# GATv2 edge scores summed by TensorE with the channels on the partitions, in a four-layer graph network on one Trainium2 core

## The chip, the core and the metric

The kernel runs on one NeuronCore of one Trainium2 chip. The metric is the device time of one execution in microseconds (us). Three runs of the kernel before are known.

## The reference, cut to what matters

3125 nodes with 256 channels, 50000 edges (sorted by target node) and one loop edge per node. Four graph layers follow one another, each with a residual sum and a layer norm. Layer 0 is the one that the change is about: two GATv2 convolutions, the first with 2 heads of 64 channels, the second with 2 heads of 128.

```python
def gatv2_conv(x, src, dst, Wl, Wr, att, b, heads, c_out):
    xl = (x @ Wl).reshape(n, heads, c_out)
    xr = (x @ Wr).reshape(n, heads, c_out)
    e = jax.nn.leaky_relu(xl[src] + xr[dst], NEG_SLOPE)      # 0.2
    logit = jnp.einsum('ehc,hc->eh', e, att)
    m = jax.ops.segment_max(logit, dst, num_segments=n)
    a = jnp.exp(logit - m[dst])
    denom = jax.ops.segment_sum(a, dst, num_segments=n)
    alpha = a / denom[dst]
    out = jax.ops.segment_sum(alpha[:, :, None] * xl[src], dst, num_segments=n)
    return out.reshape(n, heads * c_out) + b
```

Layer 1 is a GAT layer with 8 heads, layer 2 a graph transformer of three sublayers, layer 3 a sum over neighbours with a two-layer network. All arithmetic is float32.

## The kernel before, in words

The edges are first sorted into slots: 464 tiles of 128 slots, so that the two tiles of a group point to target nodes of one block of 128 nodes. `edge_pass(kind, table, width)` (L828) is then called seven times: twice as "gatv2" (pass 1 with width 128, pass 2 with width 256), once as "gat", three times as "hgt", once as "gin". A pass works through 232 groups of 2 tiles; 8 groups are a batch, of which there are 29.

The order is written out by hand. Every engine runs the same sequence of slots, one slot per group, and in slot n it does stage s for group n minus the lag of s (`LAG`): one_hots 0, turn 1, target 2, logit 3, weigh 14, add_up 15, keep 16. Once in a batch come the softmax stages LOGITS (10), IN_TILE and TURN_LOGITS (11), ACROSS (12) and POWERS (13). Engines wait for each other by semaphores, so that an engine that falls back by more than about a slot holds the others.

In a "gatv2" pass before, for each group:

- GpSimd (POOL) gathers the two tiles of source rows with an indirect DMA each (L943). It waits until the rows of two batches ago are weighed.
- VectorE (DVE) makes two one-hot tiles, slot by target node (L852).
- TensorE (PE) transposes both (L968, L969) and ScalarE (ACT) copies them to `spreads` (L1034).
- TensorE puts target row plus source row into PSUM, slots on the partitions and channels on the free axis: for each tile a matmul of `spreads` with the block's 128 target rows in `qtab` (L981) and one of the identity with the gathered rows (L984).
- ScalarE writes 0.2 times that sum to SBUF (L1039); VectorE takes the larger of both (L1124), which is the leaky relu, and then for each tile and head multiplies by `att` and sums the channels (L1187, with a second instruction that reads the accumulator).
- After the softmax, ScalarE multiplies the source rows by their weights, a tile and head at a time (L1074, four per group), and writes the weights beside them (L1080).
- TensorE sums weighted rows over the slots of each target (L1020), and VectorE adds the result to `acc` (L1213).

Once in a batch: VectorE copies the scores to `logits` (L1246), TensorE turns them (L962) so that lanes of heads and tiles lie on the partitions, VectorE runs four scans (L1148, L1149, L1165, L1167) for the maximum of each segment and subtracts it (L1177), ScalarE takes the exponential (L1050), TensorE turns the weights back (L1006). TensorE and VectorE each load 8 block numbers from `block_of` into registers.

"gat" and "hgt" passes have the same structure, but ScalarE makes the one-hots there, and VectorE weighs the rows (L1108).

Of the kernel before, what the change touches and what calls it, by code (L numbers as in the profile page):

```python
# [18 lines left out]
ALU = mybir.AluOpType  # L19
# [4 lines left out]
P = 128  # L24
# [3 lines left out]
NP = NT * P  # L28
# [11 lines left out]
BIG = 2.0 ** 100  # L40
PADSEG, PADLOC, PADDST = 9999.0, 999.0, 4000
# [23 lines left out]
def gnn_kernel(nc, A, out):  # L65

    ctx = ExitStack()
    with ctx:
# [10 lines left out]
        tab_l0a, tab_l0b, tab_l1 = dram("tab_l0a", (NP, 128)), dram("tab_l0b", (NP, D)), dram("tab_l1", (NP, D + H))  # L79
# [4 lines left out]
        seg_dram = dram("seg_dram", (1, T * P + 2))  # L84
        hid_dram = dram("hid_dram", (8, P, NP))
# [23 lines left out]
        qtab = arena[:, QTAB:QTAB + NT * D].rearrange("p (j c) -> p j c", j=NT)  # L109
# [574 lines left out]
        def load_slots():  # L684

            q4 = T // 4
            segT = arena[0:q4, 0:4 * P].rearrange("p (q s) -> p q s", q=4)
            with nc.Block() as block:
                @block.sync
                def _(sp):  # L690
                    sp.dma_start(slots_i.rearrange("p t f -> p (t f)"),
                                 rec_dram[:, :].rearrange("(p t) f -> p (t f)", p=P)).then_inc(loaded.sem, 16)
                    sp.wait_ge(placed.sem, placed.at(2))
# [5 lines left out]
                    sp.wait_ge(loaded.sem, loaded.at(16 * 7))  # L699

                @block.vector
                def _(dve):
# [6 lines left out]
                    dve.wait_ge(multiplied.sem, multiplied.at(4))  # L709
                    dve.tensor_copy(segT, PS[0][0:q4, :].rearrange("p (q s) -> p q s", q=4)).then_inc(placed.sem, 1)  # L710
                    dve.wait_ge(step.sem, step.at(5))
                    dve.wait_ge(placed.sem, placed.at(1))
# [8 lines left out]
            loaded.base += 16 * 7  # L721
            step.base += 5
            placed.base += 2
            multiplied.base += 4
# [96 lines left out]
        names = ("oh_made", "oh_turned", "spread_made", "target_spread", "activated", "leaked", "multiplied_rows", "raw_made",  # L821
# [3 lines left out]
        S = {n: sig(n) for n in names}  # L825
        arrived = [[sig(f"arrived{a}{k}") for k in range(BG)] for a in range(2)]

        def edge_pass(kind, table, width):  # L828
# [7 lines left out]
            index = slot_typed if hgt else slot_src  # L836
            pot = [PS[0][:, 0:GT * P], PS[1][:, 0:GT * P]]
            z = [PS[2][:, :].rearrange("p (t c) -> p t c", t=GT), PS[3][:, :].rearrange("p (t c) -> p t c", t=GT)]
            sums = [PS[4][:, 0:wc], PS[5][:, 0:wc]]
            plt, pcols, pscale = PS[6][:, 0:P], PS[6][:, P:P + 33], PS[6][:, 192:192 + H]  # L840
            pat = PS[7][:, 0:P].rearrange("p (h t) -> p h t", h=H)
# [4 lines left out]
            w_dve = gat or hgt  # L846
# [54 lines left out]
            with nc.Block() as block:  # L901
# [20 lines left out]
                def _(pool):  # L922
                    freed = S["summed"] if gin else S["weighted_made"]

                    def batch_fn(s, a, use):
# [8 lines left out]
                        for k in range(BG):  # L934
# [3 lines left out]
                            if not gin:  # L938
# [11 lines left out]

                @block.tensor
# [1179 lines left out]
```

## Time and profile before

| | |
|---|---|
| three runs | 8071.43, 8066.46, 8066.6 us; median 8066.6 |
| span of the profiled execution | 8071.7 us, which is taken as its own time (the profile gives no other) |
| busy share of the span | PE 75%, DVE 64%, ACT 39%, POOL 46% |
| pass 1 (gatv2, width 128), first to last scan | 943.6 to 1587.6 us |
| pass 2 (gatv2, width 256), first to last scan | 1708.5 to 2507.6 us |

Busy shares are means over stages with different limits, so the two gatv2 passes are read by themselves. Busy time of PE also overstates its load, since matmuls overlap in the pipeline: the distance between starts in the timeline is what a matmul takes from the next one. Each float32 matmul shows as two MATMUL records with two weight loads; a transpose shows as one.

### The profile page before, as it was taken

Reading aid. Unit: us, or ns where it says so; the run is one execution under the profiler, and the core shown is the slowest. Engines: PE = TensorE matmul, PEld = TensorE weight load, DVE = VectorE, ACT = ScalarE, POOL = GpSimd, SP = SyncE. Lnnn points to the kernel's source line nnn. Section 1 sums busy time; section 2 is a strip of 40 time slices with the busy share of each in tenths; the row PEclk is TensorE's granted clock in tenths of the full one; section 3 lists DMA queues with packets and bytes.
Section 4 is the critical chain, followed back from the end, with each engine's and each line's share of the span. In section 5 each row is a group of like instructions: output and inputs, shape, how many; then the busy total and the mean of one; then the engine's idle time right before and its main releaser. Section 6 shows DMA issues by size and latency. Waiting matters only on the chain. (4 is left out here: it accounts for less than half of the span.)

```text
span 8071.7 us, 142182 instructions
## 1 busy us (share of the span) xinstructions
PE 6039.7 (75%) x30254; PEld 4802.6 (59%) x30255; DVE 5203.4 (64%) x17428; ACT 3149.5 (39%) x10642; POOL 3712.1 (46%) x3878
## 2 busy tenths in 40 slices
PE   2786577778885788597887897886897886837676
PEld 1665466657774566385665785665785665724455
DVE  7664588768887566538997438997428997343313
ACT  0111266546663466325553225553225553300015
POOL 0676377545552577307662007662006662047740
PEclk9999999899997688698998999998998998955668
DMA  1000211322222233326663026663026663023330
GB/s 28 3 3 10 49 47 47 37 74 74 72 74 38 80 98 98 64 96 184 174 177 87 1 95 185 174 177 88 1 94 182 176 174 92 1 88 96 97 67 16
DMA packets 306945, 689.96 MB, mean 85 GB/s; under 512 B 95900, under 2 KB 135510, under 8 KB 306390
## 3 DMA queue, kind: packets, MB, share of 16 engines
q0 software_dynamic: 209536, 581.61, 28.1%
q1 hardware_dynamic: 81264, 98.11, 3.7%
q10 hardware_dynamic: 15846, 7.19, 0.3%
q14 instruction: 226, 1.85, 0.1%
q8 instruction: 73, 1.20, 0.1%
HBM read 605.77 MB, written 80.89 MB: 85 GB/s over the span
## 5 line engine op out<-in xcount | busy, mean ns | idle before, releaser
L943 POOL DMA_INDIRECT arena<-tab_l,idx x2320 | 2327.5, 1003 | 967.6 <-issue 578.5
L1020 PE MATMUL bank<-arena,onehots 128*128 128x264 f32 (+3 forms) x6496 | 2020.1, 443 | 340.6 <-DVE onehots L852 173.9
L981 PE MATMUL bank<-arena,spreads 128*128 x5568 | 1472.9, 373 | 609.5 <-ACT spreads L1034 251.9
L1020 PEld LDWEIGHTS bank<-arena,onehots 128*128 128x128 f32 x6496 | 1333.8, 225 | 690.4 <-issue 203.2
L981 PEld LDWEIGHTS bank<-arena,spreads 128*128 128x128 f32 x5568 | 977.3, 208 | 842.5 <-issue 776.2
L1213 DVE TENSOR_TENSOR acc<-acc,bank 128x264 f32 (+3 forms) x1624 | 657.6, 405 | 530.4 <-PE bank L1020 519.4
L1034 ACT ACTIVATE spreads<-bank 128x256 f32<-128x256 f32 x1392 | 523.0, 376 | 915.9 <-PE bank L969 912.1
L1108 DVE TENSOR_TENSOR arena<-arena,bank 128x512 f32<-128x512 f32 x928 | 631.5, 682 | 282.8 <-ACT stats L1056 140.6
L861 ACT ACTIVATE onehots<-iota_row,slot_loc 128x128 f32<-128x128 f32 x1856 | 632.3, 391 | 28.6 <-PEq L1693 24.2
L930 POOL COPY idx<-slot_typed 128x16 int32 (+1 forms) x87 | 17.6, 203 | 1328.8 <-SPq L901 1328.2
L943 POOL DMA_INDIRECT arena<-tab_l0b,idx x464 | 464.8, 1002 | 350.7 <-ACT arena L1074 192.5
L943 POOL DMA_INDIRECT arena<-tab_l0a,idx x464 | 465.4, 1003 | 192.7 <-issue 128.0
L1074 ACT ACTIVATE arena<-arena,stats 128x64 f32<-128x64 f32 (+1 forms) x1856 | 538.4, 363 | 8.7 <-PE bank L1020 3.4
L1129 DVE TENSOR_TENSOR bank<-bank,arena 128x512 f32<-128x512 f32 x696 | 485.3, 697 | 33.6 <-DMA arena<-tab_l,idx 31.1
L645 POOL DMA_INDIRECT rec_dram<-arena x417 | 409.4, 982 | 193.2 <-issue 125.9
L984 PE MATMUL bank<-arena,ident 128*128 128x128 f32 (+1 forms) x1856 | 485.6, 346 | 0.0
L968 PE MATMUL bank<-ident,onehots 128*128 128x128 f32 x1392 | 423.6, 304 | 79.5 <-ACT onehots L865 43.7
L1196 DVE TENSOR_REDUCE raw<-bank 128x16 f32<-128x512 f32 x696 | 476.6, 685 | 3.8
L852 DVE TENSOR_SCALAR onehots<-iota_row,slot_loc 128x128 f32<-128x128 f32 x1392 | 351.6, 310 | 137.0 <-PE bank L1020 95.5
L1187 DVE CUSTOM_DVE_ANT_0 bank<-bank,att 128x64 f32<-128x64 f32 (+1 forms) x1856 | 423.3, 291 | 12.1
L1039 ACT ACTIVATE arena<-bank 128x256 f32<-128x256 f32 (+1 forms) x464 | 226.9, 489 | 461.8 <-PE bank L984 459.6
L969 PE MATMUL bank<-ident,onehots 128*128 128x128 f32 x1392 | 405.9, 292 | 0.0
(331 smaller groups left out, 9936.6 us busy)
## 6 DMA issues: line engine op xcount, KB each, us to landing
tab_l<-arena SPq DMA_DIRECT2D x75, 768.0 KB, 3.5
arena<-tab_l,idx POOLq DMA_INDIRECT x2320
arena<-tab_l0a,idx POOLq DMA_INDIRECT x464
arena<-tab_l0b,idx POOLq DMA_INDIRECT x464
rec_dram<-arena POOLq DMA_INDIRECT x417, 2.1
tab_l<-arena SPq DMA_DIRECT2D x25, 132.0 KB, 1.7
tab_l0b<-arena SPq DMA_DIRECT2D x25, 128.0 KB, 1.7
residual<-X SPq DMA_DIRECT2D x1, 3200.0 KB
```

The lines of the kernel that those rows point to most:

```text
L861: act.activation(onehots[:, x.a, t, :], iota_row[:, :], ACT.Abs, scale=-1.0, bias=loc[:, ds(BT * x.batch + t, 1)]).then_inc(S["distance"]. ...
L943: pool.indirect_dma_start(out=rows_sb[:, a, t, 0:width], out_offset=None, in_=table[:, :], in_offset=bass.IndirectOffsetOnAxis(ap=idx[:, a ...
L968: pe.transpose(pot[x.k % 2][:, 0:P], onehots[:, x.a, GT * x.k, :], ident[:, :])
L981: mm = pe.matmul(z[x.k % 2][:, t, 0:cw], spreads[:, x.k % 2, t * P:t * P + P], qtab[:, block_no[w % BG], 0:cw], start=True, stop=not gatv2)
L984: mm = pe.matmul(z[x.k % 2][:, t, 0:cw], ident[:, :], rows_sb[:, x.a, GT * x.k + t, 0:cw], start=False, stop=True)
L1020: mm = pe.matmul(sums[x.k % 2], onehots[:, x.a, GT * x.k + t, :], rhs, start=t == 0, stop=t == GT - 1)
L1034: act.activation(spreads[:, x.k % 2, :], pot[x.k % 2], ACT.Copy)\
L1074: op = act.activation(wt[:, t, lanes, 0:C], rows_sb[:, x.a, GT * x.k + t, h * cw // 2:(h + 1) * cw // 2] .rearrange("p (r c) -> p r c", r= ...
L1108: dve.tensor_tensor(wt[:, :, :, 0:C], lane_split(src, C), p.unsqueeze(3).to_broadcast([P, GT, H, C]), ALU.mult)\
L1129: dve.tensor_tensor(pr, pr, src[:, :, 0:D], ALU.mult).then_inc(S["multiplied_rows"].sem, 1)
L1196: dve.tensor_reduce(r, lane_split(pr, C), AX, ALU.add).then_inc(S["raw_made"].sem, 1)
L1213: dve.tensor_tensor(av, av, sums[x.k % 2], ALU.add).then_inc(S["added_up"].sem, 1)
```

## The change

Only the two gatv2 passes compute in another way; the other five passes keep their instructions.

- **Scores with channels on the partitions.** TensorE forms the sum of target row and source row transposed: for each block of 128 channels (`kb` is 1 in pass 1 and 2 in pass 2) one matmul of the target rows with the spread matrix of both tiles (256 columns), and one per tile of the source rows with the identity (128 columns). ScalarE copies the sum and its relu to `bent`. Leaky relu is 0.2 x + 0.8 relu(x), so TensorE gets the score with one matmul per tile, channel block and part (128 columns each), whose weights are the attention vector times 0.2 or 0.8 at the columns of this tile's lanes and zero elsewhere (`flat_mask` in `att`, `bent_mask` in `vecs`). All matmuls of a batch add up in one PSUM bank, which the scans read.
- **Spread matrix without TensorE.** The slots' target numbers are stored to DRAM (`loc_dram`) once; SP loads 16 x 128 of them for a batch, the same to all 128 partitions (1 MB), and VectorE compares them with the partition number, one instruction per batch. Both transposes of a group and ScalarE's copy go.
- **Target rows by DMA.** `project` stores target rows in the second half of the table in DRAM, and SP loads the block of each group (64 or 128 KB). TensorE no longer loads block numbers in these passes.
- **VectorE weighs the rows**, one instruction per group, as in gat and hgt; ScalarE's four per group go. VectorE's maximum, its sums over channels, the copy to `logits` and TensorE's turn of them go.

The diff, cut to its core:

```diff
@@ load_slots
+                        sp.dma_start(loc_dram[0, q * q4 * P:(q + 1) * q4 * P].rearrange("(t s) -> t s", s=P),
+                                     locT[:, q, :]).then_inc(loaded.sem, 16)
@@ edge_pass
-            w_dve = gat or hgt
+            w_dve = not gin
...
+                @block.sync
+                def _(sp):
+                    def batch_fn(s, a, use):
+                        if needed(BG * (s - 1)):
+                            sp.wait_ge(S["target_spread"].sem, S["target_spread"].at(BG * (s - 1)))
+                            sp.sem_inc(tick.sem, 1)
+                        sp.dma_start(spread_of[:, a, :, :],
+                                     loc_dram[0:1, ds(BT * P * s, BT * P)].to_broadcast([P, BT * P])
+                                     .rearrange("p (t s) -> p t s", t=BT)).then_inc(loc_in[a].sem, 16)
+                        block_no = next_blocks(mybir.EngineType.SP, 0, BG * s)
+                        for k in range(BG):
+                            if needed(BG * (s - 2) + k + 1):
+                                sp.wait_ge(S["target_spread"].sem, S["target_spread"].at(BG * (s - 2) + k + 1))
+                                sp.sem_inc(tick.sem, 1)
+                            sp.dma_start(targets[:, a, k, :], table[ds(block_no[k] * P + NP, P), :])\
+                              .then_inc(target_in[a][k].sem, 16)
...
@@ tensor, slot_fn
+                        x = Group(i, w, LAG["logit"])
+                        if x.there and gatv2:
+
+                            pe.wait_ge(S["activated"].sem, S["activated"].at(2 * (x.g + 1)))
+                            if x.k == 0 and needed(x.batch - 1):
+                                pe.wait_ge(S["shifted_made"].sem, S["shifted_made"].at(x.batch - 1))
+                            for t in (GT * x.k, GT * x.k + 1):
+                                for k in range(kb):
+                                    for b, mask in enumerate((flat_mask, bent_mask)):
+                                        mm = pe.matmul(plt[x.a], mask[:, k, BT - 1 - t:BT - 1 - t + P],
+                                                       bent[x.k % 2][:, b, k, t % 2 * P:t % 2 * P + P],
...
+                            mm.then_inc(S["scored"].sem, 1)
+                            for k in range(kb):
+                                pe.matmul(zT[x.k % 2][:, k, :], targets[:, x.a, x.k, k * P:k * P + P],
+                                          spread_of[:, x.a, GT * x.k:GT * x.k + GT, :], start=True, stop=False)
+                                for t in range(GT):
+                                    mm = pe.matmul(zT[x.k % 2][:, k, t * P:t * P + P],
+                                                   rows_sb[:, x.a, GT * x.k + t, k * P:k * P + P], ident[:, :],
+                                                   start=False, stop=t == GT - 1)
+                            mm.then_inc(S["target_spread"].sem, 1)
@@ scalar, slot_fn
-                            act.activation(rows_sb[:, x.a, GT * x.k:GT * x.k + GT, D:D + cw], z[x.k % 2][:, :, 0:cw],
-                                           ACT.Copy, scale=0.2)\
+                            if needed(x.g - 1):
+                                act.wait_ge(S["scored"].sem, S["scored"].at(x.g - 1))
+                            act.activation(bent[x.k % 2][:, 0, :, :], zT[x.k % 2], ACT.Copy)\
+                               .then_inc(S["activated"].sem, 1)
+                            act.activation(bent[x.k % 2][:, 1, :, :], zT[x.k % 2], ACT.Relu)\
                                .then_inc(S["activated"].sem, 1)
@@ vector, slot_fn
+                        if x.there and gatv2 and x.k == 0:
+                            dve.wait_ge(loc_in[x.a].sem, loc_in[x.a].at(16 * (x.use + 1)))
+                            dve.tensor_scalar(spread_of[:, x.a, :, :], spread_of[:, x.a, :, :], small[:, 0:1], None,
+                                              ALU.is_equal).then_inc(S["spread_made"].sem, 1)
@@ layer_0
+            def masks(dve, link, lanes):
+
+                for v, slope in ((att, 0.2), (vecs[:, 512:1024], 0.8)):
+                    link(dve.memset(v[:, 0:2 * MASK], 0.0))
```

TensorE's order in pass 2, inside the loop. Before, one slot from the sum over slots (L1020) to the next; `arena` stands for the target rows and the gathered rows:

```order
L1020 MATMUL bank<-arena,onehots 128x264 x2
L965 REGISTER_ALU
L968 MATMUL bank<-ident,onehots 128x128
L969 MATMUL bank<-ident,onehots 128x128
L981 ISA
L981 MATMUL bank<-arena,spreads 128x256
L984 MATMUL bank<-arena,ident 128x256
L981 MATMUL bank<-arena,spreads 128x256
L984 MATMUL bank<-arena,ident 128x256
L1014 REGISTER_ALU
L1017 REGISTER_ALU
L1020 MATMUL bank<-arena,onehots 128x264 x2
```

Now, from the last two score matmuls of one group (L1022; `att` and `vecs` are the two masks, and the pair stands four times in a slot) through the next group's sums (L1035, L1038) and the sum over slots (L1079) to the next scores:

```order
L1022 MATMUL bank<-arena,att 128x128
L1022 MATMUL bank<-arena,vecs 128x128
L1035 MATMUL bank<-arena 128x256
L1038 MATMUL bank<-ident,arena 128x128 x2
L1035 MATMUL bank<-arena 128x256
L1038 MATMUL bank<-ident,arena 128x128 x2
L1079 MATMUL bank<-arena,onehots 128x264 x2
L1016 ISA
L1022 MATMUL bank<-arena,att 128x128
L1022 MATMUL bank<-arena,vecs 128x128
```

Two transposes left the slot, eight float32 matmuls of 128 columns came in, and between a group's sums and its scores stands the sum over slots alone.

ScalarE's order in pass 2, one slot, before:

```order
L1031 REGISTER_ALU
L1034 ACTIVATE spreads<-bank 128x256
L1039 ACTIVATE arena<-bank 128x2x256
L1074 ACTIVATE arena<-arena,stats 128x4x32 x4
L1080 ACTIVATE arena<-stats 128x2x8
```

and now:

```order
L1097 REGISTER_ALU
L1100 ACTIVATE arena<-bank 128x512
L1102 ACTIVATE arena<-bank 128x512
L1124 REGISTER_ALU
L1130 ACTIVATE arena<-stats 128x2x8
```

The copy to `spreads` and the four weighings left; the relu (L1102) came in behind the copy (L1100), and TensorE's scores wait for both.

## Rows read from the trace of the kernel before

**Rows 1.** The page, busy time of each engine over the whole span
```profile
PE 6039.7 (75%) x30254; PEld 4802.6 (59%) x30255; DVE 5203.4 (64%) x17428; ACT 3149.5 (39%) x10642; POOL 3712.1 (46%) x3878
```
**Rows 2.** Windows: from:to length, busy (count), PE clock, DMA share, GB/s; passes 1, 2
```profile
943.60:1587.60 644.00, 477.00 (x3274) 424.15 (x3274) 517.87 (x3180) 400.70 (x1635) 449.23 (x470) 0.92 0.24 46
1708.50:2507.60 799.10, 701.88 (x3274) 579.95 (x3272) 667.21 (x3179) 494.71 (x1634) 446.68 (x468) 0.97 0.29 73
```
**Rows 3.** By source line, the batch's first scan: durations ns, first and last start
```profile
L1148 DVE TENSOR_TENSOR_SCAN arena<-bars,bank x29: 399/409/420, 943.6 to 1587.6; 128x128 f32<-128x128 f32 x29
...
L1148 DVE TENSOR_TENSOR_SCAN arena<-bars,bank x29: 405/411/422, 1708.5 to 2507.6; 128x128 f32<-128x128 f32 x29
```
**Rows 4.** Timeline of PE in pass 2, one slot: start, duration, line [idle before]
```profile
2061.05 0.60 PE L981 MATMUL bank<-arena,spreads 128*128 x2
2061.49 0.59 PE L984 MATMUL bank<-arena,ident 128*128 128x256 f32 x2
...
2062.78 1.05 PE L1020 MATMUL bank<-arena,onehots 128*128 128x264 f32 x4
2063.67 0.27 PE L968 MATMUL bank<-ident,onehots 128*128 128x128 f32 x1
...
2063.89 0.60 PE L981 MATMUL bank<-arena,spreads 128*128 x2
```
**Rows 5.** Timeline of PE in pass 1
```profile
1254.12 0.63 PE L1020 MATMUL bank<-arena,onehots 128*128 128x136 f32 x4
1254.59 0.27 PE L968 MATMUL bank<-ident,onehots 128*128 128x128 f32 x1
...
1254.81 0.39 PE L981 MATMUL bank<-arena,spreads 128*128 x2
1255.03 0.39 PE L984 MATMUL bank<-arena,ident 128*128 128x128 f32 x2
```
**Rows 6.** Timeline of PE in layer 2's perceptron: 16 float32 matmuls of 128 columns
```profile
4454.94 3.74 PE L1872 MATMUL bank<-spreads,arena 128*128 128x128 f32 x32
4458.52 1.68 PE L1881 MATMUL bank<-arena 128*128 128x256 f32 x7
```
**Rows 7.** Timeline of ACT: a reader of TensorE's sums, and two in a row
```profile
2062.98 0.60 ACT L1039 ACTIVATE arena<-bank 128x512 f32<-128x512 f32 x1 [0.98 <-PE bank L984]
...
6029.72 1.08 ACT L1774 ACTIVATE onehots<-bank 128x512 f32<-128x512 f32 x2 [0.87 <-PE bank L1732]
```
**Rows 8.** Timeline of ACT and PE: TensorE waits for ScalarE
```profile
2074.82 0.36 ACT L1034 ACTIVATE spreads<-bank 128x256 f32<-128x256 f32 x1
...
2075.25 0.69 PE L981 MATMUL bank<-arena,spreads 128*128 x2 [1.14 <-ACT spreads L1034]
```
**Rows 9.** Groups of instructions in pass 1, 930 to 1560 us
```profile
L1039 ACT ACTIVATE arena<-bank 128x256 f32<-128x256 f32 x221 | 84.1, 381 | 176.2 <-PE bank L984 175.5 <-issue 0.6
```
**Rows 10.** Timeline of POOL around a batch's end
```profile
2062.58 1.00 POOL L943 DMA_INDIRECT arena<-tab_l0b,idx  x1 [2.77 <-ACT arena L1074]
2063.88 1.00 POOL L943 DMA_INDIRECT arena<-tab_l0b,idx  x1 [0.31 <-issue]
...
2066.24 1.02 POOL L943 DMA_INDIRECT arena<-tab_l0b,idx  x1 [1.15 <-DVE raw L1187]
```
**Rows 11.** Timeline of DVE, the stage ACROSS of a batch in pass 1
```profile
1589.49 0.19 DVE L1161 TENSOR_TENSOR carried<-bank,tile_border 128x33 f32<-128x33 f32 x1 [0.31 <-PE bank L990]
...
1591.04 0.29 DVE L1177 TENSOR_TENSOR arena<-bank,seg_max 128x128 f32<-128x128 f32 x1
```
**Rows 12.** Groups of DVE: pass 2, 1700 to 2480 us, and the weighing in hgt
```profile
L1187 DVE CUSTOM_DVE_ANT_0 bank<-bank,att 128x128 f32<-128x128 f32 x877 | 228.8, 323 | 5.6
L1124 DVE TENSOR_TENSOR bank<-bank,arena 128x512 f32<-128x512 f32 x219 | 152.3, 695 | 0.5 <-ACT arena L1039 0.3
...
L1108 DVE TENSOR_TENSOR arena<-arena,bank 128x512 f32<-128x512 f32 x928 | 631.5, 682 | 282.8 <-ACT stats L1056 140.6
```
**Rows 13.** DMA queues: packets, MB, share of 16 engines; 818 to 840, 1250 to 1273 us
```profile
q1 hardware_dynamic: 4800, 1.93, 102.9%
...
q0 software_dynamic: 529, 1.11, 18.7%
```

More of the change, by code:

```diff
@@ L720, in _ @@
                           .then_inc(multiplied.sem, 1)
-            loaded.base += 16 * 7
+                        pe.transpose(PS[1][0:q4, q * P:q * P + P], slots[:, q * q4:(q + 1) * q4, 3], ident[:, :])\
+                          .then_inc(multiplied.sem, 1)
+            loaded.base += 16 * 11
             step.base += 5
-            placed.base += 2
-            multiplied.base += 4
+            placed.base += 3
+            multiplied.base += 8
         def find_borders():
@@ L825, in gnn_kernel @@
         S = {n: sig(n) for n in names}
+        loc_in = [sig("loc_in0"), sig("loc_in1")]
+        target_in = [[sig(f"target_in{a}{k}") for k in range(BG)] for a in range(2)]
         arrived = [[sig(f"arrived{a}{k}") for k in range(BG)] for a in range(2)]
@@ L957, in slot_fn @@
                         x = at_batch(i, w, TURN_LOGITS)
-                        if x and not gin:
+                        if x and (gat or hgt):
                             pe.wait_ge(S["logits_made"].sem, S["logits_made"].at(x.batch + 1))
@@ L961, in slot_fn @@
                                 pe.wait_ge(S["scale_in"].sem, S["scale_in"].at(x.batch))
-                            pe.transpose(plt, logits[:, :], ident[:, :]).then_inc(S["logits_turned"].sem, 1)
+                            pe.transpose(plt[0], logits[:, :], ident[:, :]).then_inc(S["logits_turned"].sem, 1)
                         x = Group(i, w, LAG["turn"])
-                        if x.there and not gin:
+                        if x.there and (gat or hgt):
                             pe.wait_ge(S["oh_made"].sem, S["oh_made"].at(x.g + 1))
@@ new lines, in slot_fn @@
+                        x = Group(i, w, LAG["target"])
+                        if x.there and gatv2:
+                            pe.wait_ge(S["spread_made"].sem, S["spread_made"].at(x.batch + 1))
+                            if needed(2 * (x.g - 1)):
+                                pe.wait_ge(S["activated"].sem, S["activated"].at(2 * (x.g - 1)))
+                            pe.wait_ge(arrived[x.a][x.k].sem, arrived[x.a][x.k].at(32 * (x.use + 1)))
+                            pe.wait_ge(target_in[x.a][x.k].sem, target_in[x.a][x.k].at(16 * (x.use + 1)))
+                            for k in range(kb):
[6 more added lines that the diff above has]
+                            mm.then_inc(S["target_spread"].sem, 1)
+                        elif x.there and not gin:
@@ L1029, in slot_fn @@
                         x = Group(i, w, LAG["turn"])
-                        if x.there:
+                        if x.there and not gatv2:
                             act.wait_ge(S["oh_turned"].sem, S["oh_turned"].at(x.g + 1))
@@ L1120, in slot_fn @@
                         src = rows_sb[:, xl.a, GT * xl.k:GT * xl.k + GT, :]
-                        if xl.there and gatv2:
-                            dve.wait_ge(S["activated"].sem, S["activated"].at(xl.g + 1))
-                            dve.tensor_tensor(pr, pr, src[:, :, D:D + cw], ALU.max).then_inc(S["leaked"].sem, 1)
-                        elif xl.there and not gin:
+                        if xl.there and (gat or hgt):
                             dve.wait_ge(S["target_spread"].sem, S["target_spread"].at(xl.g + 1))
@@ L1273, in edge_pass @@
             if gatv2:
-                per_group += ("activated", "leaked")
+                per_group += ("activated", "activated", "scored")
+                S["spread_made"].base += NB
+                for a in range(2):
+                    loc_in[a].base += 16 * ((NB + 1 - a) // 2)
+            else:
+                if not gin:
+                    per_group += ("raw_made", "oh_turned", "spread_made")
+                    S["logits_made"].base += NB
+                    S["logits_turned"].base += NB
             if hgt:
```

150 lines of the change are left out of this document (74 added, 76 removed).

## The prediction

> **What bounds the kernel now.** The busy shares of the span [rows 1] name no engine that is full, and they mix seven passes. The change touches two of them, so I read those by themselves. The by-line view of the batch's first scan gives the period: 28 intervals in 644.0 us, or **23.0 us per batch** of 8 groups, in pass 1, and 28 in 799.1 us, or **28.5 us**, in pass 2 [rows 3].
>
> In pass 2 the timeline of TensorE is to be read by its starts. A 256-column float32 matmul (two records) takes 0.43 us from the next, the sum over slots 0.89 (2062.78 to 2063.67), each transpose 0.11, and the slot repeats after 2.84 us without a gap [rows 4]. TensorE alone sets that slot. Eight of them are 22.7 us; the other 5.8 us of a batch are stretches in which VectorE's batch stages and the register loads hold both engines. VectorE is nearly full too: 667.21 us busy in 28 batches is 23.8 us of 28.5 [rows 2].
>
> In pass 1 TensorE's slot has 1.57 us of work: 0.47 for the sum over slots, 0.22 for transposes, four matmuls of 128 columns at 0.22 [rows 5]. The bound is near POOL: a gather every 1.30 us, and 2.36 once a batch where it copies the indices [rows 10], so 15 x 1.30 + 2.36 = 21.9 us per batch of 23.0.
>
> **The change, part by part, pass 2.**
>
> *TensorE loses* two transposes (0.22 us) and the 1.74 us of the old sums. *It gets* for the new sums, for each of two channel blocks, one matmul of 256 columns (0.43) and two of 128 columns (0.22 each): 1.74 us, no change. *It gets* 8 score matmuls of 128 columns. The nearest row is the perceptron's: 16 such matmuls, each with new weights, in 4458.52 - 4454.94 = 3.58 us, or 0.224 each [rows 6]. That is 1.79 us. The sum over slots stays, 0.89. TensorE's work in a slot goes from 2.84 to 4.42 us. That alone exceeds the old 28.5 / 8 = 3.57 us, stalls included.
>
> *A new wait.* TensorE sums group g, does the sum over slots of an older group, and then needs copy and relu of g for its scores. ScalarE starts 0.20 us after TensorE has moved on (2062.98 against 2062.78), two activations of 512 columns take 1.08 us [rows 4, 7], and TensorE resumes 0.07 us after ScalarE ends (2074.82 + 0.36 against 2075.25) [rows 8]: 1.35 us, of which the sum over slots covers 0.89. So 0.46 us of each slot is idle, with the next sums and the following groups queued behind it. The slot is 1.74 + 1.35 + 1.79 = **4.88 us**. The ends are 4.42 (all hidden) and 5.15 (the handoffs cost double).
>
> *Per batch*: 8 x 4.88 = 39.0, plus 0.3 for three small matmuls on TensorE = 39.3 us against 28.5, so +10.8 us, x 29 = **+313 us**. I count nothing for the old 5.8 us of stalls: TensorE has no register load any more, and VectorE has room. It loses 0.70 for the maximum and four times about 0.25 for the channel sums (the instruction is 0.32 alone, its accumulator read overlaps), gets 0.68 for weighing [rows 12], and once a batch a compare of 2048 elements (16 tiles; not more than 16 x 0.31 = 5 us by the mean of a one-hot tile, 2 to 3 by elements). 23.8 - 13.6 + 5.4 + 3 is 18.6 us of 39.3. If this cover failed, VectorE's stalls would cost up to 5.8 x 29 = 168 us; I keep a third of it for the upper end.
>
> **Pass 1.** New sums 0.43 + 2 x 0.22 = 0.87, scores 4 x 0.224 = 0.90, sum over slots 0.47. ScalarE's pair of 256 columns is 0.38 [rows 9] plus 0.26 (a second one costs 0.12 less, as in rows 7), so the wait is 0.20 + 0.64 + 0.07 = 0.91. The slot is 2.68 us, 21.4 per batch, + 0.3. One wait shows here: at POWERS TensorE needs VectorE's scale and the last weighing of the batch before, which VectorE does only after its chain of scans, 1.84 us from 1589.49 to 1591.04 + 0.29 [rows 11]. I work out 1.2 us of stall from it, and in pass 2 none, because its slots are longer. 22.9 us per batch against 23.0, and POOL's 21.9 beneath: **0 us** (-32 if POOL alone binds, +60 if the waits are larger).
>
> **Outside the batches**: four more stores and transposes of slot numbers, two chains of six small instructions for the masks, stores of twice the size in two projections, and in each pass the first 1 MB load ahead of the first compare. I take **+15 us**, ends 0 and 35.
>
> **DMA** I cost at nothing. Per batch there come 1 MB of slot numbers and 0.5 or 1 MB of target rows. They are issued about seven slots ahead, and the queues' share is 0.24 and 0.29 now [rows 2].
>
> **TensorE's clock.** It was granted at 0.92 and 0.97 of 2.4 GHz on average [rows 2], and all my durations are from stretches at the full level. The change takes away the batch-wise gaps, so I sum at 1.00. The Trainium skill ("TensorE: Matmul & The Clock Gate", Part 1: The HAM clock gate) says that half rate is the default and that activity releases it; by it the clock would also stay up here. If instead it stayed at 0.97, pass 2 would take 3% of 39.3 x 29, or 34 us more, which is within the range.
>
> **Sum.** 313 + 0 + 15 = +328 us. Against the profiled execution's 8071.7 us that is 8400; that execution is 5 us above the median of 8066.6, so the median should be **8395 us**, 4.1% slower.
>
> **Rivals.**
>
> A. *The forecast*: pass 2 runs at TensorE's 4.88 us. For it: the slot of rows 4 has no gap already, and work is added to it. Chance 0.77.
>
> B. *Handoff hidden*: ScalarE's pair fits under the sum over slots and TensorE's 4.42 us bind. 0.46 x 8 x 29 = 107 us less, 8288. Against it: 0.20 + 1.08 is longer than 0.89 whatever the order. Chance 0.06.
>
> C. *DMA becomes the bound of pass 1.* The one load of 520-byte pieces in the trace kept all 16 queues full for about 22 us for 1.93 MB [rows 13]. At that rate 1 MB takes 11.7 us per batch, the target rows of pass 1 5.9, and the gathers have 0.24 x 23 = 5.5: 23.1 us of 23.0, so the gathers come late. With 4 us per batch that is +116, 8511. It decides once the loads cost more than some 15 us of all queues per batch. Against it: these pieces are whole 512 bytes, and pass 2 has 39 us for 31.7. The Trainium skill ("DMA: Bandwidth & Descriptors", Issuing engines are not separate DMA queues) says that DMAs of all issuing engines interleave on the same 16 engines, which speaks for C. Chance 0.13.
>
> D. *Faster*: VectorE and ScalarE were what held pass 2, and the scores are nearly free on TensorE. The slot would be 1.74 + 1.35 = 3.09, 25.0 per batch, -102; pass 1 falls to POOL's 21.9, -32; with +15 that is 7948. It turns the sign only if the 8 score matmuls take under 0.48 us instead of 1.79. Rows 6 speak against it. Chance 0.03; 0.01 is left for a result that nothing distinguishes.
>
> **How the numbers follow.** The predicted time is A's. A's own ends are the handoff (+62), pass 1 (-32, +60), the stalls (+56), the clock and what lies outside; they do not all fall together, so A spans about 8330 to 8480. The range takes in C's 8511 and half of B: **8300 to 8520**. A difference under 0.2% (16 us) is what a measurement of this kernel can't tell from none. Faster 0.03, same 0.01, slower 0.96.
>
> **What would show it.** In pass 2: scans 39 us apart; the scores' records 0.11 us apart; ScalarE waiting for TensorE's sums nearly always; a gap of 0.4 to 0.5 us before the first score matmul, put down to ScalarE; clock at 1.00; VectorE busy under half. In pass 1: scans 23 us apart, POOL with few waits. Wrong would be: scans of pass 2 under 35 us apart (scores cheaper than rows 6), or waits for the loads of slot numbers or target rows (C).

## The result, and the profile after

| | before | changed |
|---|---|---|
| median of 4 runs | 8069.02 us (8066.46 to 8073.16) | **8431.45 us** (8429.5 to 8437.88) |
| span of the profiled execution | 8071.7 us | 8436.0 us |

The ratio is **1.0449, 95% interval [1.0434, 1.0464]**: 362 us slower. The forecast was 8395 us in a range of 8300 to 8520, and slower with a chance of 0.96.

The page's busy times of the changed kernel answer to [rows 1]. TensorE gained 507 us and VectorE lost 349, ScalarE 439; POOL changed by 31.

```profile
PE 6547.1 (78%) x35304; PEld 5260.0 (62%) x35305; DVE 4854.0 (58%) x13728; ACT 2710.7 (32%) x8786; POOL 3743.0 (44%) x3878
```

The batch's first scan by source line, changed kernel, passes 1 and 2, answers to [rows 3]:

```profile
L1201 DVE TENSOR_TENSOR_SCAN arena<-bars,bank x29: 407/412/421, 951.9 to 1610.3; 128x128 f32<-128x128 f32 x29
```
```profile
L1201 DVE TENSOR_TENSOR_SCAN arena<-bars,bank x29: 410/411/419, 1748.5 to 2869.1; 128x128 f32<-128x128 f32 x29
```

Pass 1 takes 658.4 us over 28 intervals, 23.5 a batch, and pass 2 1120.6 us, **40.0 a batch** (23.0 and 28.5 before). The 364.3 us between the two spans are then 14.4 in pass 1, **321.5 in pass 2**, and 28.4 outside: 8.3 ahead of the first scan, 17.3 between the passes, 2.8 behind. The stretch between the passes holds the first groups of pass 2, which run ahead of its first scan. The last projection matmul and the first matmul of pass 2, before and changed (timelines of PE):

```profile
1671.03 0.67 PE L1467 MATMUL bank<-arena,spreads 128*128 128x512 f32 x1 [0.38 <-DVE arena L1567]
...
1684.08 0.47 PE L968 MATMUL bank<-ident,onehots 128*128 128x128 f32 x1 [11.95 <-DVE onehots L852]
```
```profile
1691.10 0.67 PE L1516 MATMUL bank<-arena,spreads 128*128 128x512 f32 x1 [0.38 <-DVE arena L1631]
...
1706.53 1.22 PE L1035 MATMUL bank<-arena 128*128 128x256 f32 x2 [14.34 <-DVE arena L1168]
```

From its first matmul to its first scan pass 2 takes 24.4 us before (1684.08 to 1708.5) and 42.0 changed (1706.53 to 1748.5): 17.6 more. So **339 us of the 364 are pass 2's**, 14.4 lie between pass 1's scans, and 10.8 are left for all the rest.

The windows of the two passes (length, busy time of PE, PEld, DVE, ACT, POOL, clock, DMA share, GB/s) answer to [rows 2]:

```profile
951.90:1610.30 658.40, 582.27 (x4160) 520.94 (x4158) 375.25 (x1384) 192.96 (x754) 456.87 (x467) 1.00 0.44 109
1748.50:2869.10 1120.60, 1064.18 (x7296) 934.95 (x7294) 467.94 (x1385) 288.59 (x754) 458.33 (x458) 1.00 0.35 101
```

VectorE is busy 16.7 us of a batch of 40.0 in pass 2, where it had 23.8 of 28.5. The clock is at 1.00 in both passes. The DMA share has risen from 0.24 to 0.44 in pass 1 and from 0.29 to 0.35 in pass 2.

One slot of pass 2 on the timeline of PE, changed kernel (answers to [rows 4]):

```profile
2209.63 1.06 PE L1079 MATMUL bank<-arena,onehots 128*128 128x264 f32 x4
2210.97 0.49 PE L1022 MATMUL bank<-arena,att 128*128 128x128 f32 x2 [0.28 <-ACT arena L1102]
2211.29 0.39 PE L1022 MATMUL bank<-arena,vecs 128*128 128x128 f32 x2
...
2212.86 0.60 PE L1035 MATMUL bank<-arena 128*128 128x256 f32 x2
...
2214.61 1.06 PE L1079 MATMUL bank<-arena,onehots 128*128 128x264 f32 x4
```

From one sum over slots to the next are 4.98 us. From its start to the first score matmul pass 1.34 (2209.63 to 2210.97), of which it fills 0.89 by itself, so 0.45 is the handoff. The scores take 1.89 (to 2212.86): seven at 0.22, and the first, which has stood waiting, 0.32. The sums take 1.75 (to 2214.61). Who waits for whom is plain in the groups of instructions, both passes, 900 to 2900 us (busy us, mean ns, idle us before, releasers):

```profile
L1022 PE MATMUL bank<-arena,att 128*128 128x128 f32 x2784 | 583.7, 291 | 125.8 <-ACT arena L1102 120.2 <-ACT arena L1100 2.3
...
L1100 ACT ACTIVATE arena<-bank 128x256 f32<-128x256 f32 (+1 forms) x464 | 227.5, 490 | 1298.7 <-PE bank L1038 1286.9 <-issue 10.1
...
L1168 DVE TENSOR_SCALAR arena<-arena,small 128x2048 f32<-128x2048 f32 x58 | 74.4, 1284 | 4.0 <-DMA arena<-loc_dram 3.9
```

ScalarE waits 1287 us for TensorE's sums, TensorE 120 for ScalarE's relu (its line of score matmuls was idle for 125.8 in all, in 464 groups, 0.27 each; the rest of the 0.45 by the starts goes to the weight load, which waits too), and VectorE 3.9 for the load of slot numbers.

In pass 1 TensorE's slot is 2.78 us, and once a batch TensorE waits for VectorE (timeline of PE; answers to [rows 5] and [rows 11]):

```profile
1257.74 0.60 PE L1035 MATMUL bank<-arena 128*128 128x256 f32 x2
...
1258.62 0.63 PE L1079 MATMUL bank<-arena,onehots 128*128 128x136 f32 x4
1259.53 0.49 PE L1022 MATMUL bank<-arena,att 128*128 128x128 f32 x2 [0.28 <-ACT arena L1100]
1259.85 0.39 PE L1022 MATMUL bank<-arena,vecs 128*128 128x128 f32 x2
...
1260.52 0.60 PE L1035 MATMUL bank<-arena 128*128 128x256 f32 x2
...
1264.60 0.39 PE L1058 MATMUL bank<-head_rhs,ones 128*128 128x8 f32 x2 [0.25 <-DVE head_rhs L1270]
1265.39 0.33 PE L1065 MATMUL bank<-ident,arena 128*128 128x128 f32 x1 [0.41 <-DVE arena L1158]
```

### The profile page after: what moved, and what is told of

Its sections match the earlier page's. It is cut to its first block and busy times, and to the rows that moved or that the text cites. A ratio compares the mean times of both kernels' runs of the same rounds, so it can differ in the third digit from the quotient of the medians.

```text
span 8436.0 us, 149914 instructions
## 1 busy us (share of the span) xinstructions
PE 6547.1 (78%) x35304; PEld 5260.0 (62%) x35305; DVE 4854.0 (58%) x13728; ACT 2710.7 (32%) x8786; POOL 3743.0 (44%) x3878
## 5 line engine op out<-in xcount | busy, mean ns | idle before, releaser
L1079 PE MATMUL bank<-arena,onehots 128*128 128x264 f32 (+3 forms) x6496 | 2002.6, 440 | 330.6 <-DVE onehots L872 173.8
L1079 PEld LDWEIGHTS bank<-arena,onehots 128*128 128x128 f32 x6496 | 1303.1, 222 | 666.6 <-issue 205.1
L1047 PE MATMUL bank<-arena,spreads 128*128 x3712 | 961.2, 380 | 330.1 <-DVE raw L1239 183.7
L1158 DVE TENSOR_TENSOR arena<-arena,bank 128x512 f32<-128x512 f32 (+1 forms) x1392 | 882.6, 635 | 486.7 <-ACT stats L1118 318.6
L1047 PEld LDWEIGHTS bank<-arena,spreads 128*128 128x128 f32 x3712 | 653.9, 209 | 494.5 <-issue 432.9
L1022 PE MATMUL bank<-arena,att 128*128 128x128 f32 x2784 | 583.7, 291 | 125.8 <-ACT arena L1102 120.2
L1093 ACT ACTIVATE spreads<-bank 128x256 f32<-128x256 f32 x928 | 353.1, 381 | 912.6 <-PE bank L1009 909.7
L1100 ACT ACTIVATE arena<-bank 128x256 f32<-128x256 f32 (+1 forms) x464 | 227.5, 490 | 1298.7 <-PE bank L1038 1286.9
L881 ACT ACTIVATE onehots<-iota_row,slot_loc 128x128 f32<-128x128 f32 x1856 | 632.2, 391 | 28.5 <-PEq L1757 24.3
L1022 PEld LDWEIGHTS bank<-arena,att 128*128 128x128 f32 x2784 | 420.9, 191 | 260.4 <-ACT arena L1102 240.6
L1022 PE MATMUL bank<-arena,vecs 128*128 128x128 f32 x2784 | 539.3, 275 | 0.0
L1035 PE MATMUL bank<-arena 128*128 128x256 f32 x1392 | 419.3, 383 | 33.8 <-DVE arena L1168 29.2
L1038 PEld LDWEIGHTS bank<-ident,arena 128*128 128x128 f32 x2784 | 422.6, 192 | 36.4
```

The costliest lines, as they stand in the source:

```text
L881: act.activation(onehots[:, x.a, t, :], iota_row[:, :], ACT.Abs, scale=-1.0, bias=loc[:, ds(BT * x.batch + t, 1)]).then_inc(S["distance"]. ...
L1022: mm = pe.matmul(plt[x.a], mask[:, k, BT - 1 - t:BT - 1 - t + P], bent[x.k % 2][:, b, k, t % 2 * P:t % 2 * P + P], start=t == 0 and k == 0 ...
L1035: pe.matmul(zT[x.k % 2][:, k, :], targets[:, x.a, x.k, k * P:k * P + P], spread_of[:, x.a, GT * x.k:GT * x.k + GT, :], start=True, stop=False)
L1038: mm = pe.matmul(zT[x.k % 2][:, k, t * P:t * P + P], rows_sb[:, x.a, GT * x.k + t, k * P:k * P + P], ident[:, :], start=False, stop=t == G ...
L1047: mm = pe.matmul(z[x.k % 2][:, t, 0:cw], spreads[:, x.k % 2, t * P:t * P + P], qtab[:, block_no[w % BG], 0:cw], start=True, stop=True)
L1079: mm = pe.matmul(sums[x.k % 2], onehots[:, x.a, GT * x.k + t, :], rhs, start=t == 0, stop=t == GT - 1)
```

## The experiments

They ran on three chips. On the first (e1 to e4) the kernel before took 9463.44 us, on the second (f1 to f4) 9335.16, on the third (g1 to g4) 8070.61, like the chip of the prediction. Times are only compared with the kernel before on the same chip; durations of instructions agree on all three. What differs in the pages is how much data moves in a time, the GB/s in the 40 slices, the changed kernel on the chip of the prediction and on the second:

```profile
GB/s 27 3 3 23 101 112 112 82 118 105 110 101 103 50 71 98 98 65 101 182 175 175 53 18 133 181 175 168 15 44 152 177 176 140 0 68 95 97 72 15
```
```profile
GB/s 24 2 2 2 53 86 87 87 91 95 101 104 104 76 48 75 74 72 65 132 142 141 128 13 71 144 141 142 103 2 116 136 141 141 66 21 95 90 84 14
```

Where the later passes gather most, the one moves up to 182 GB/s and the other 144. Why those chips are slower is not shown: the rate would also fall if something else took longer, and TensorE's granted clock over the whole profiled execution is lower there too, 0.81 in f1 against 0.885.

**The base.** f1 and g2 are the changed kernel, unaltered, g1 the kernel before.

> The changed kernel itself, as the base for the runs beside it. In the four runs before, the chip was slower for the kernel before too (9463 us), with gathers that moved about 140 GB/s where the first chip moved about 180. Theory (TensorE's slot sets pass 2): the ratio to the kernel before is 1.04 to 1.05 on a chip like the first; on a chip with slow transfers the slot is still 4.98 us where no transfer is late, and the ratio is 1.02 to 1.05. Rival (the loads of slot numbers and target rows set the loss): on a chip with slow transfers the ratio is above 1.06.

> The changed kernel as the base for the two runs behind it. 1.03 to 1.05 of the kernel before; slot of pass 2 4.98 us on any chip, since no transfer is in it.

> The kernel before itself, for its profile on the same chip as the runs beside it. If the chip is one with slow gathers (about 140 GB/s), pass 1 takes 28 to 30 us per batch as in all runs there whatever the kernel, so the loss of the changed kernel lies in pass 2, where the kernel before should take 29 to 31 us per batch against 40.6. Rival (the loads make the loss there): pass 1 of the kernel before is much nearer to the 23.0 us of the first chip.

f1: 9655.25 us, ratio 1.0331 [1.0311, 1.0351]. g2: 8432.85 us, ratio **1.0448 [1.0430, 1.0465]**. g1: 8064.19 us in one run, 22.9 and 28.6 us per batch in passes 1 and 2, so it repeats the kernel before and not its loss on a chip with slow gathers. f1's pass 1 took 29.8 us a batch and its pass 2 40.6; g2's 23.5 and 40.0. Pass 2 of the changed kernel hardly depends on the chip, pass 1 does. The kernel before has no profile from the second chip. The nearest is f4 below, 52 us slower than it: 30.0 us a batch in pass 1, no less than f1's 29.8, and 32.5 in pass 2. So on that chip the loss lies in pass 2 as well. It is smaller there (320 us for 362), which would fit if the kernel before loses time to late rows in its pass 2 that the longer slots of the changed kernel hide; this was not measured.

**The handoff: e1 and f2**, one more group between sums and scores.

```
+            if gatv2:
+                LAG.update(logit=4)
```

> The changed kernel with the score stage one slot later (lag 4 in place of 3): ScalarE then has a whole slot for copy and relu. Theory H (the handoff from TensorE to ScalarE and back costs 0.46 us of each slot plus 0.10 us for the first matmul after the wait): pass 2's slot falls from 4.98 to 4.42 us, its batch from 40.0 to about 35.5; pass 1's falls from 23.5 to POOL's 21.9 to 22.3. In all -165 to -175 us, about 8260. Rival V (the wait shown at the scores only covers another engine's lateness, VectorE's or a load's): pass 2 stays within 1 us of 40.0 per batch, in all less than 40 us gained.

> One more group between sums and scores, beside the changed kernel on the same chip. Theory: the handoff of 1.34 us is hidden behind the next group's sums, the slot of pass 2 goes from 4.98 to 4.43 us, pass 2 from 40.0 to about 35.7 us per batch (-125 us), pass 1 by 0 to 50 us, in all -125 to -175 us against the changed kernel, so still 1.02 to 1.03 of the kernel before. Rival: the wait only moves on, less than 40 us gained.

e1: 9567.46 us, ratio 1.0108 [1.0085, 1.0131]; pass 2 took 35.9 us a batch, close to the 35.5 expected, and pass 1 28.5, not the 21.9 to 22.3 expected from the first chip's rows. f2: 9479.03 us, ratio 1.0151 [1.0134, 1.0168], **176 us under f1** on the same chip: pass 2 at 35.8 us a batch against 40.6, 4.77 x 28 = 134, pass 1 at 28.4 against 29.8, 38. A slot of f2 on the timeline of PE:

```profile
2303.03 1.06 PE L1081 MATMUL bank<-arena,onehots 128*128 128x264 f32 x4
2303.92 0.38 PE L1024 MATMUL bank<-arena,att 128*128 128x128 f32 x2
...
2305.70 0.60 PE L1037 MATMUL bank<-arena 128*128 128x256 f32 x2
...
2307.46 1.06 PE L1081 MATMUL bank<-arena,onehots 128*128 128x264 f32 x4
```

4.43 us and no gap: 0.45 of waiting and 0.10 of the first matmul behind the wait are gone, 0.55 x 8 = 4.4 us a batch. f2 saved 4.8 us a batch in pass 2. The rival, a wait that only moves on, has fallen. TensorE's bare work, 4.43, is what the prediction summed to 4.42, and it is still more than the 3.57 of the kernel before with its stalls.

**The scores: e2**, half of them left out.

```
-                                    for b, mask in enumerate((flat_mask, bent_mask)):
+                                    for b, mask in enumerate((flat_mask,)):
```

> The changed kernel without the second score matmul of each pair: the relu part is left out of the scores, all else stays, ScalarE's relu too. Theory S (each float32 score matmul of 128 columns costs its 0.224 us on the path): pass 2's slot 4.98 to 4.08 us, batch 32.9; pass 1's slot would be 2.41, so POOL's 21.9 to 22.3 per batch bind there. In all about -245 us, 8185. Rival (scores are partly covered, another engine is close behind): less than half of that.

9607.19 us, one run, 1.0152 of the kernel before; against f1's ratio, which is from another chip, that is 1.8%, about 170 us, less than the 245 expected and more than the rival's half. Pass 1 stayed at 29.8 us a batch, where 21.9 to 22.3 was expected. The slot shows what pass 2 gained (timeline of PE, and the windows of one stretch, e2):

```profile
2405.29 1.06 PE L1079 MATMUL bank<-arena,onehots 128*128 128x264 f32 x4
2406.62 1.16 PE L1022 MATMUL bank<-arena,att 128*128 128x128 f32 x8 [0.28 <-ACT arena L1102]
...
2409.38 1.06 PE L1079 MATMUL bank<-arena,onehots 128*128 128x264 f32 x4
...
2524.30 1.16 PE L1022 MATMUL bank<-arena,att 128*128 128x128 f32 x8 [0.65 <-ACT arena L1102]
2530.96 1.81 PE L1022 MATMUL bank<-arena,att 128*128 128x128 f32 x8 [2.85 <-ACT arena L1102]
2536.77 1.15 PE L1022 MATMUL bank<-arena,att 128*128 128x128 f32 x8 [0.36 <-ACT arena L1102]
```
```profile
2530.96:2534.90 3.94, 3.94 (x16) 3.66 (x17) 0.51 (x3) 0.07 (x1) 1.99 (x2) 0.57 0.92 266
```

Where nothing else is late the slot is 4.09 us: 0.89 less than 4.98 for four score matmuls, **0.22 each**. But two slots of this batch are 6.66 and 5.81 us long, and the mean batch is 36.7 us where 8 x 4.09 is 32.7. The first has a gap of 2.85 us, which comes when the row gathers of a new batch have started late. That the gathers cause it is read from the order of the rows, and was not tried by itself. The second has hardly a gap: behind the long one TensorE ran at a granted clock of 0.57 for 3.94 us, mostly the lower level of 1.2 GHz, and its eight records took 1.81 us instead of 1.16.

**The loads: e3 and g3.** e3 loads one tile of slot numbers in 16; g3 cuts the target rows too.

```
+                        tiles = BT if isinstance(s, int) and s < 2 else 1
-                        sp.dma_start(spread_of[:, a, :, :], ...
+                        sp.dma_start(spread_of[:, a, 0:tiles, :], ...
...
+                            rows = P if isinstance(s, int) and s < 2 else 8
-                            sp.dma_start(targets[:, a, k, :], table[ds(block_no[k] * P + NP, P), :])\
+                            sp.dma_start(targets[0:rows, a, k, :], table[ds(block_no[k] * P + NP, rows), :])\
```

> The changed kernel in which from the third batch on only one of the 16 tiles of slot numbers is loaded (64 KB in place of 1 MB a batch); the spread matrix of the others is what is left in the buffer, so the target part of the scores is wrong. Theory A (the loads cost nothing beside TensorE's work): within 10 us of the changed kernel. Rival C (DMA holds pass 1): 50 to 116 us faster, nearly all of it in pass 1.

> Both new loads cut from the third batch on: the slot numbers to one tile of 16, the target rows to 8 of 128 (scores are then of stale rows). 1.4 MB less per batch of pass 2. Theory (TensorE's slot sets pass 2, the loads are hidden): pass 2 within 0.5 us per batch of the changed kernel; on a chip with slow gathers pass 1 may fall by up to 1.5 us per batch, so 0 to 50 us in all. Rival C (the loads crowd the gathers): 60 to 200 us faster than the changed kernel.

e3: 9791.53 us, ratio 1.0339 [1.0315, 1.0363], no less than f1's 1.0331 on a chip that is slow too; the changed kernel was not run on e3's chip, so 10 us could not be told there. g3: 8430.21 us, ratio 1.0445 [1.0427, 1.0462], beside g2's 8432.85 on the same chip. The windows of g3 between the times at which the changed kernel has its scans (g3's own are at 953.1 to 1608.1 and 1744.4 to 2864.9), columns as above:

```profile
951.90:1610.30 658.40, 582.86 (x4174) 522.43 (x4174) 377.47 (x1393) 192.97 (x754) 458.28 (x468) 1.00 0.23 48
1748.50:2869.10 1120.60, 1062.92 (x7282) 933.23 (x7280) 470.34 (x1391) 287.56 (x753) 458.35 (x458) 1.00 0.20 54
```

The DMA share falls from 0.44 to 0.23 and from 0.35 to 0.20, and the passes stay at 23.4 and 40.0 us a batch. Rival C has fallen for this chip: taking the new loads away gains 2.6 us of 8433, less than the runs spread. For the slow chips only e3 speaks, which left the target rows in.

**Half of the scores, at another price: e4 and f3.** The maximum of z and 0.2 z on VectorE needs one mask and one score matmul for a channel block and tile; with the longer lag.

```
-                            act.activation(bent[x.k % 2][:, 0, :, :], zT[x.k % 2], ACT.Copy)\
-                            act.activation(bent[x.k % 2][:, 1, :, :], zT[x.k % 2], ACT.Relu)\
+                            act.activation(bent[x.k % 2][:, 1, :, :], zT[x.k % 2], ACT.Copy, scale=0.2)\
...
+                            dve.tensor_tensor(bent[x.k % 2][:, 0, :, :], zT[x.k % 2], bent[x.k % 2][:, 1, :, :],
+                                              ALU.max).then_inc(S["leaked"].sem, 1)
```

> A version that may beat both: ScalarE writes 0.2 z, VectorE takes the larger of z and 0.2 z (one instruction per group), so one score matmul per tile and block is enough, and the scores come at lag 4. If TensorE alone binds: pass 2's slot 1.74 + 0.90 + 0.89 = 3.53 us, batch 28.5, pass 1 at POOL's 22, in all about 8060. Rival: VectorE has 0.48 + 0.68 + 0.70 + 0.43 = 2.3 us a slot and some 10 us a batch, 28.3 us of 28.5, so that the batch stages stall TensorE: batch 31 to 33 in pass 2, 8130 to 8190.

> One score matmul for each channel block instead of two, on the maximum of z and 0.2 z that VectorE takes, with the longer lag. Theory: TensorE's slot of pass 2 is 4.43 - 0.90 = 3.53 us or a little more where VectorE is in the way, 30 to 33 us per batch, so 210 to 290 us under pass 2 of the changed kernel and the whole at 0.99 to 1.01 of the kernel before. Rival (VectorE or ScalarE bind at once): pass 2 above 35 us per batch, 1.02 or more.

e4: 9462.79 us, ratio 1.0000 [0.9987, 1.0012]. f3: 9338.31 us, ratio **1.0005 [0.9993, 1.0016]**, 317 us under f1. Its slot is 3.54 us without a gap (2406.56 to 2410.10 below), pass 2 is 31.4 us a batch (predicted 30 to 33), so 258 us less, and pass 1 is 28.0, 50 less. So half the scores and the hidden handoff win back nearly the whole loss, and no more. e4's pass 2 took 32.8 us a batch: in both runs pass 2 came out where e4's rival had it, with VectorE's batch stages stalling TensorE, though the totals are near its theory's (8060 us of 8067, or 0.999). Of the 3 us of a batch above 8 x 3.54, 1.6 are waits for VectorE in f3 (44 us in all of pass 2: 18.6 for its sums in `acc`, 18.3 for the last weighing, 7.3 for its scale). At one batch (f3, timeline of PE):

```profile
2401.79 0.39 PE L1060 MATMUL bank<-head_rhs,ones 128*128 128x8 f32 x2 [0.70 <-DVE head_rhs L1275]
2402.85 0.33 PE L1067 MATMUL bank<-ident,arena 128*128 128x128 f32 x1 [0.67 <-DVE arena L1158]
...
2406.56 1.06 PE L1081 MATMUL bank<-arena,onehots 128*128 128x264 f32 x4
...
2410.10 1.06 PE L1081 MATMUL bank<-arena,onehots 128*128 128x264 f32 x4
```

**Weighing on ScalarE again: g4**, on top of f3.

```
-            w_dve = not gin
+            w_dve = gat or hgt
```

(with the four activations per group and the wait for `powers_kept` of the kernel before)

> The version with the maximum on VectorE and the longer lag, with the weighing of rows given back to ScalarE, which was busy 178 of 878 us there. Theory: its slot of pass 2 is TensorE's 3.54 us and 8 of them are 28.3; of the 3.0 us of stalls in a batch those at the transposed powers (1.4 us, TensorE waits for VectorE's scale and its last weighing) go for the greater part, so pass 2 falls from 31.4 to about 29 to 30 us per batch, 30 to 70 us in all: 0.993 to 0.998 of the kernel before. Rival (ScalarE then hands the scores' input on late): no gain or slower than the kernel before.

8143.36 us, ratio 1.0091 [1.0074, 1.0108]: slower than before, where 0.993 to 0.998 was expected. f3 was not run on this chip, so what the weighing alone does to the total is not measured. Pass 2 did what it should, 28.95 us a batch, 0.4 more than the kernel before (28.6). **Pass 1** did not: 25.0 us against 22.9 is 60 us of the 73. The waits of g4 in pass 1, 1000 to 1600 us, and POOL at a batch's end:

```profile
PE bank L1037 <- DMA arena<-tab_l0a,idx: 130.3, 62, 5.7
...
POOL arena L965 <- ACT arena L1140: 86.5, 64, 3.2
```
```profile
1212.35 1.10 POOL L965 DMA_INDIRECT arena<-tab_l0a,idx  x1 [1.05 <-ACT arena L1140]
1213.75 1.00 POOL L965 DMA_INDIRECT arena<-tab_l0a,idx  x1 [0.30 <-issue]
```

TensorE waits for gathered rows 62 times, 130 us in all, and only once, for 0.3 us, for the maximum that feeds the scores, so it is not the rival's mechanism. POOL issues the gathers 1.30 to 1.40 us apart, once ScalarE's weighing has freed a buffer. Added up over pass 1 from the rows of POOL, it is busy for 16.8 us a batch, takes 4.4 between instructions, and stands 3.4 before the weighing, 24.6 of 25.0. In the kernel before it was busy for 16.0, took 4.4 and stood 2.2, 22.6 of 23.0. So a quicker TensorE slot gains nothing there: TensorE waits for rows, whose gathers take POOL 21.2 us of a batch and then wait for buffers that the weighing frees. Of the 2.0 us more, 0.8 are longer gathers, of which the last section tells, and 1.2 a longer wait for the weighing. Why the weighing frees the buffers later was not tried: the longer lag keeps the distance from the weighing to the sums, but it brings the last scores of a batch one slot nearer to its scans.

**Weighing alone: f4**, the kernel before with `w_dve = not gin`, ScalarE's four activations taken out, and TensorE's wait ahead of the transposed powers as in gat and hgt.

> The kernel before with only the weighing of rows moved from ScalarE to VectorE, nothing else of the change. Theory: VectorE has 23.8 us of work in a batch of 28.5 in pass 2 and 18.5 of 23.0 in pass 1; weighing adds 8 x 0.68 = 5.4 and 8 x 0.38 = 3.0 us, so pass 2 is then VectorE's at 29.2 us plus stalls, 31 to 34 us per batch (+70 to +160 us), pass 1 23 to 24 (0 to +30): 8140 to 8260 us on the first chip, ratio 1.01 to 1.023. So this part alone would not have been free, and it is free in the changed kernel only since VectorE is relieved of the score sums. Rival (weighing is cheap anywhere): within 0.4% of the kernel before.

9387.56 us, ratio 1.0055 [1.0038, 1.0073], 52 us slower. Its passes, pass 2 first, columns as above:

```profile
2214.30:3123.30 909.00, 738.83 (x3275) 597.21 (x3274) 785.58 (x3401) 256.09 (x750) 440.41 (x458) 0.95 0.24 63
1227.60:2067.90 840.30, 550.13 (x3277) 498.52 (x3275) 571.81 (x3401) 206.68 (x751) 438.82 (x458) 0.78 0.16 35
```

VectorE is busy 785.6 us of 909.0 in pass 2, 28.1 of 32.5 a batch, within the 31 to 34 expected. The whole cost, 0.55%, is less than the 1% to 2.3% of the theory and more than the 0.4% of the rival. The theory's size was for the first chip, and the run does not decide on it: pass 1 took 30.0 us a batch here, where 23 to 24 was expected, so other waits may cover part of the cost. Its sign is sure: the weighing is not free on a VectorE as full as before.

## Why the prediction was right

**What bounds.** That TensorE's work and its one wait set the slot of pass 2 in the changed kernel is shown. Taking the wait (f2) or matmuls (e2, f3) off TensorE shortens the slot by just their starts' distance; taking bytes away (g3) does nothing. The words "TensorE alone sets that slot" were said of the kernel before, where they rest on the rows without a gap and were not tried.

**Scores**, 0.224 each, 1.79 a slot: 0.22 in the timeline, and 0.89 for four in e2. The rows of the perceptron [rows 6] gave the right price.

**The new wait**, 1.35 us from the sum over slots to the scores: 1.34. Rival B, a hidden handoff, did not come, as forecast, and f2 shows what it would have been worth: 134 us of pass 2 on its chip, for the 107 of the rival's sum, since the restart goes too. **Mis-sized** was the slot, 4.88 for 4.98: the first matmul behind the wait costs 0.32 us, not 0.22, a restart that the sum left out. 0.10 x 8 = 0.8 us a batch explains 40.0 against 39.3.

**The old stalls**, 5.8 us a batch counted as gone: 8 x 4.98 = 39.8 of 40.0, so they are. Not all of them were what the prediction said, batch stages and register loads. In some batches part was TensorE's lower clock behind a gap (kernel before, timeline and window of PE):

```profile
2056.25 1.22 PE L981 MATMUL bank<-arena,spreads 128*128 x2 [2.02 <-issue]
...
2059.66 0.29 PE L995 MATMUL bank<-head_rhs,ones 128*128 128x8 f32 x2
```
```profile
2056.20:2059.70 3.50, 3.45 (x10) 2.80 (x11) 3.07 (x16) 0.72 (x4) 1.89 (x2) 0.53 0.12 34
```

At a granted clock of 0.53, near the 1.2 GHz level, the sums took 3.41 us instead of 1.74. By the mean of 0.97 over pass 2 [rows 2] this is, as an estimate, 0.03 x 28.5 = 0.9 of the 5.8 us. The compare of 2048 elements took 1.28 us, not 2 to 3.

**Pass 1**, "0 us": +14.4. From the sum over slots to the scores pass 0.91 us as forecast, and the restart adds its 0.10 here too, so the slot is 2.78 for 2.68, 0.8 us a batch more. The stall at POWERS was 1.2 us in the sum and is 0.25 + 0.41 in the rows, which takes a part of it back. Most batches take 23.3 us; the first two and the last two, at 24.3 to 25.9, make the mean 23.5 for 22.9. The sum's two misses here, 0.8 too little and 0.5 too much, cancel in part.

**Outside**, +15. Of the 28.4 us outside the spans of scans, 17.6 are pass 2's first groups, which the sum had counted as its 29th batch. That leaves 10.8. The first load and compare ahead of pass 2, which the sum names, cost 2.4 of them (15.4 us from the last projection matmul to the first sum, for 13.1).

The sum was +328 for +364.3. Pass 2 has 339 for 313, the restart above all (0.8 x 29 = 23 us); pass 1 has 14.4 for 0; what lies outside has 10.8 for 15.

**Rival C** fell with g3. Its price was too high: it gave the new loads 17.6 us of all queues per batch of pass 1 (11.7 + 5.9), and they take 5.5, 23.5% of 23.5 us (changed kernel, the queue of both loads, 1000 to 1600 us):

```profile
q1 hardware_dynamic: 32336, 38.81, 23.5%
```

The load of 520-byte pieces [rows 13] was no measure for them. In the trace the slot numbers move in pieces of 8192 bytes, not of 512 as the prediction has it, and cost 3.3 us a batch for its 11.7; the target rows of pass 1 do move in pieces of 512 and cost 2.0 for its 5.9.

**Rival D** fell with the slot's rows and with e2: the scores took 1.79 us, not under 0.48.

**The clock** was granted at 1.00 in both passes, the level 2.4 GHz, as summed; the means before were 0.92 and 0.97.

## What to carry to other kernels

Where one engine's slot has no gap, a change that relieves two other engines and adds to that one costs what it adds to the slot: 8 matmuls of 0.22 us cost 1.8 us here. What it wins back are the stalls between slots, 5.8 us a batch here, which the 2.14 us more in each of 8 slots outweigh. A handoff through another engine inside a slot costs its whole round trip less what stands between, plus the restart; one more group of distance took it away (176 us of the 320 lost on that chip). Look after each such step at what is next: with TensorE quick enough, pass 1 went by the gathers and the buffers they wait for (g4), and no version beat the kernel before.

## What the runs showed of the hardware

A gather on POOL takes 1.00 us to issue, and 1.38 to 2.04 where it meets VectorE's compare of 2048 elements (changed kernel, timelines of POOL and DVE at the start of pass 2 and inside it):

```profile
1704.00 1.00 POOL L963 DMA_INDIRECT arena<-tab_l0b,idx  x1 [0.30 <-issue]
1705.30 2.04 POOL L963 DMA_INDIRECT arena<-tab_l0b,idx  x1 [0.30 <-issue]
...
1713.00 1.88 POOL L963 DMA_INDIRECT arena<-tab_l0b,idx  x1 [0.31 <-issue]
...
2212.68 1.77 POOL L963 DMA_INDIRECT arena<-tab_l0b,idx  x1 [5.30 <-DVE arena L1158]
```
```profile
1705.19 1.29 DVE L1168 TENSOR_SCALAR arena<-arena,small 128x2048 f32<-128x2048 f32 x1
...
1712.72 1.29 DVE L1168 TENSOR_SCALAR arena<-arena,small 128x2048 f32<-128x2048 f32 x1 [3.11 <-DMA arena<-loc_dram]
...
2213.05 1.28 DVE L1168 TENSOR_SCALAR arena<-arena,small 128x2048 f32<-128x2048 f32 x1
```

In 26 of 29 batches of pass 1 the gather beside the compare takes 1.38 or 1.39 us, in 26 of pass 2 1.76 to 1.78, and in all of these it ends 0.12 to 0.14 us behind the compare. Gathers of the two passes that meet no compare take at most 1.13 us, and in the kernel before, which has no such compare, 1.13 too (1.18 in g1). The Trainium skill ("SBUF — State Buffer", Who interferes with whom) says that an instruction of VectorE in a mode with two ports blocks GpSimd for its whole length and not by a share. The rows agree, in that no such gather ended while the compare ran: 1.04 and 0.88 us more beside an instruction of 1.29 that began 0.11 and 0.28 earlier. That the compare is in such a mode no row here says. In pass 2 the gather is held although it began first, by 0.37 us.

The first float32 matmul of 128 columns after a wait for ScalarE took 0.32 us to the next one where all others took 0.22, in 353 of the 355 places in the changed kernel (profile after) at which such a wait is shown: 0.32 or 0.33 there, 0.59 in the other two.

The changed kernel took 8431.45 and 8432.85 us on one kind of chip and 9655.25 on another, with the same durations of instructions; why is not shown.
